# A transformer block with conditioned norm: attention rebuilt batch by batch, scores as fp32 matmuls in four row tiles, and their burst placed ahead of an output projection

## What is computed

```python
emb = silu(sin_emb(timestep)) @ W_ada + b_ada
scale, shift = split(emb[:, None, :], 2, axis=-1)
x = ln(src) * (1.0 + scale) + shift
q, k, v = heads(x @ Wq + bq), heads(x @ Wk + bk), heads(x @ Wv + bv)
scores = einsum('bhqd,bhkd->bhqk', q / sqrt(32), k) + attention_bias   # bias: 64 x 16 x 128 x 128
scores = where(src_mask, -inf, scores)
ctx = merge(einsum('bhqk,bhkd->bhqd', softmax(scores), v))
x = x + (ctx @ Wo + bo)
h = ln(x) * g2 + beta2
out = x + (gelu2(h @ W1 + b1) @ W2 + b2)
```

## Time and profile before

| | |
|---|---|
| median of 3 runs | 2750.17 us (2747.64 to 2753.22) |
| span of the profiled execution | 2749.9 us |
| PE / DVE / ACT / POOL busy | 2608.5 / 1646.0 / 1152.7 / 889.7 us |
| mean granted TensorE clock | 0.991 |
| attention stage, 134 to 1182 us | 28 pairs; DMA engines 58% busy |
| last residual add of attention | 1273.24 us |
| first feed-forward matmul | 1277.87 us |

### The profile page before, as it was taken

How to read it: one execution, slowest core, us unless ns; L and a number is a source line. 1 busy time by engine, 2 the same in 40 slices (tenths; PEclk the granted TensorE clock), 3 DMA queues, 4 the chain that set the end, 5 groups by cost and what they waited for, 6 DMA issues and landing times.

```text
span 2749.9 us, 47237 instructions
## 1 busy us (share of the span) xinstructions
PE 2608.5 (95%) x15386; PEld 2152.0 (78%) x15386; DVE 1646.0 (60%) x3087; ACT 1152.7 (42%) x3625; POOL 889.7 (32%) x767
## 2 busy tenths in 40 slices
PE   5899999999999999987999999999999999999999
PEld 3778777877777878776888888788887887878887
DVE  6899999999999999995423332332233323322322
ACT  3667777767776767774321122112211221112111
POOL 3666666666666666662000000000000000000000
PEclk8999999999999999998999999999999999999999
DMA  6556555556555556553200000000000000000000
GB/s 183 144 155 167 155 144 149 160 155 167 153 146 149 158 156 166 153 151 96 73 20 31 32 14 18 32 31 14 18 31 32 13 19 32 31 10 22 31 16 16
DMA packets 307526, 236.72 MB, mean 86 GB/s; under 512 B 27808, under 2 KB 265504, under 8 KB 303328
## 3 DMA queue, kind: packets, MB, share of 16 engines
q1 hardware_dynamic: 307424, 235.22, 30.5%
HBM read 151.01 MB, written 33.82 MB: 67 GB/s over the span
## 4 chain that ended last, share of the span: by engine, by line
PE 52%; DVE 1%; issue 0%; ACT 0%; DVEq 0%
PE psH L1088 9%; PE psH L1090 9%; PE psH L1089 9%; PE psY L1088 8%; PE psY L1090 8%; PE psY L1089 8%; PE turn L201 1%; DVE hT_hi L219 0%; DVE hT_lo L222 0%; ACT gf L1021 0%; DVE wo_hi L1046 0%; DVE r L1063 0%; DVE w_lo L1053 0%; ACT w_hi L1026 0%; DVEq L953 0%
## 5 line engine op out<-in xcount | busy, mean ns | idle before, releaser
L1021 ACT ACTIVATE gf<-psH,b_c 128x512 f32<-128x512 f32 x256 | 176.2, 688 | 1184.2 <-PE psH L1090 1184.2
L1046 DVE CAST wo_hi<-gf 128x512 fp32r<-128x512 f32 x256 | 109.6, 428 | 925.4 <-ACT gf L1021 925.4
L650 ACT ACTIVATE s<-s,nmx 128x128 f32<-128x128 f32 x1024 | 398.6, 393 | 162.3 <-DVE nmx L715 161.3
L1088 PE MATMUL psH<-hT_hi,w_hi 128*128 128x512 f32 x1024 | 405.9, 396 | 7.3 <-DVE w_lo L1053 5.1
L1088 PE MATMUL psY<-w_hi,wo_hi 128*128 128x512 f32 x1024 | 410.4, 401 | 0.0
L1090 PE MATMUL psH<-hT_hi,w_lo 128*128 128x512 f32 x1024 | 406.0, 396 | 0.0
L1089 PE MATMUL psH<-hT_lo,w_hi 128*128 128x512 f32 x1024 | 405.4, 396 | 0.0
L1090 PE MATMUL psY<-w_hi,wo_hi 128*128 128x512 f32 x1024 | 405.0, 396 | 0.0
L1089 PE MATMUL psY<-w_lo,wo_hi 128*128 128x512 f32 x1024 | 404.4, 395 | 0.0
L586 POOL TENSOR_TENSOR s<-s,rinv 128x512 f32<-128x512 f32 x256 | 266.4, 1040 | 422.8 <-DVE rinv L721 422.8
L580 POOL TENSOR_TENSOR bias<-bias,mneg 128x512 f32<-128x512 f32 x256 | 329.8, 1288 | 2.1 <-DVE mneg L726 2.1
(11 more groups left out here) (152 smaller groups left out, 5356.5 us busy)
## 6 DMA issues: line engine op xcount, KB each, us to landing
bias<-in_bias SPq DMA_DIRECT2D x128, 512.0 KB, 4.9
adab<-ada_rows SPq DMA_DIRECT2D x32, 1024.0 KB, 6.1
kbd<-kT SPq DMA_DIRECT2D x256, 128.0 KB, 2.6
xin<-in_x SPq DMA_DIRECT2D x32, 512.0 KB, 3.8
kbd<-kT SPq DMA_DIRECT2D x256, 64.0 KB, 2.3
resid<-rout SPq DMA_DIRECT2D x64, 256.0 KB, 3.0
r<-resid SPq DMA_DIRECT2D x16, 1024.0 KB, 5.6
out<-r SPq DMA_DIRECT2D x64, 256.0 KB, 2.2
```

The source lines that it names most:

```text
L650: last = act.activation(s[:, g % 2, j, :], s[:, g % 2, j, :], ACT.Exp, bias=nmx[:, g % 2, j:j + 1], accum_out=sums[:, g % 2, j:j + 1])
L1021: act.activation(gf[:, j % 2, :], psH[j % 2][:, :], ACT.Gelu_apprx_sigmoid, bias=b1_c[:, j:j + 1]).then_inc(gelu_done, 1)
L1046: dve.tensor_copy(gT[0][:, j % 2, :], gf[:, j % 2, :]).then_inc(g_hi, 1)
L1088: pe.matmul(out_ap, sh, mh, start=start, stop=False)
```

## The change

Attention goes batch by batch (`t`, 64 of them), a step has all four head groups of one batch, and the loop turns over four pairs. What is different:

- Scores: `kf` and `qf` stay fp32. The columns of Wq and Wk (and of bq, bk) are permuted in the setup, so that partitions 32i to 32i+31 of chunk a hold head 4i + a. `qk` is one burst of 16 fp32 matmuls for a whole batch, contraction 32, with a row tile position i * 32, four row tiles in turn, each to its own PSUM bank psS[i]. `kbd`, `kT`, `qT`, their splits, memsets and the SP transfers are gone. The burst of batch t+1 stands in PE's order behind the V projection and ahead of the output projection of batch t-1.
- The transposes of p go to the same four banks psS, after the scores of the next batch have been read from them; `psP` is gone. p·v is one burst for all 16 heads.
- First norm: gain and shift are applied by POOL (`residual`) and the transposes take that `xres`; from PSUM ACT makes the high part in one copy and DVE the low part in one subtraction. Gains come batch by batch (`load_gains`), x and its normalized form further ahead. The turned gains `adaT` and their transposes in the setup are gone.
- bo is no longer in the shift: POOL adds it to the rows of the feed-forward block (`add_bo`, four per group), and the statistics of the second norm wait for it.
- The weight splits for Q and K in the setup are four instructions each with permuted columns instead of one, and bq and bk arrive in four small transfers each.

```diff
+    def residual(self, pool, q, slot, b):
+        out = self.xres[:, slot, b, :]
+        at_least(pool, self.xn_ready, q * 2 + (b + 1))
+        at_least(pool, self.adab_in[b], (q + 1) * DMA)
+        pool.tensor_tensor(out, self.xn[:, b, :], self.adab[:, b, 0:self.DM], ALU.mult).then_inc(self.res_half, 1)
+        at_least(pool, self.res_half, q * 2 + (b + 1))
+        pool.tensor_tensor(out, out, self.adab[:, b, self.DM:], ALU.add).then_inc(self.res_ready, 1)
...
+    def transpose(self, pe, q, slot, b):
+        at_least(pe, self.res_ready, q * 2 + (b + 1))
+        at_least(pe, self.x_split, q * 2 + b)
...
+    def high(self, act, q, u, b):
         at_least(act, self.xt_done, q * 2 + (b + 1))
+        act.activation(self.xT[u][0][:, :, b * P:(b + 1) * P], self.psX[:, :, :], ACT.Copy).then_inc(self.x_hi, 1)
+    def low(self, dve, q, u, b):
         at = slice(b * P, (b + 1) * P)
+        at_least(dve, self.x_hi, q * 2 + (b + 1))
+        dve.tensor_tensor(self.xT[u][1][:, :, at], self.psX[:, :, :], self.xT[u][0][:, :, at].bitcast(F32),
+                          ALU.subtract).then_inc(self.x_split, 1)
...
+    def add_bo(self, pool, n, u, b):
+        at_least(pool, self.r_in[u], ((n - u) // 2 + 1) * DMA)
+        pool.tensor_tensor(self.r[u][:, b, :], self.r[u][:, b, :], self.bo_bc[:, :], ALU.add).then_inc(self.bo_added, 1)
     def statistics(self, dve, n, u, b):
-        at_least(dve, self.r_in[u], ((n - u) // 2 + 1) * DMA)
+        at_least(dve, self.bo_added, n * self.NB + (b + 1))
         dve.bn_stats(self.st[:, b, :], self.r[u][:, b, :]).then_inc(self.bn_done, 1)
...
-            def spread_k(q, b):
...
+                t = p * 2 + b
+                if on.done:
+                    store(t - 2, b)
+                if on.bias:
+                    load_bias(t + 2, p + 1, b)
+                if on.load:
+                    norm.load(sp, p + 4, u % 2)
+                if on.gains:
+                    norm.load_gains(sp, ada_rows, p + 3, b)
...
+            def step(p, u, b, on):
+                t = p * 2 + b
+                if on.turn:
+                    norm.residual(pool, p + 2, (u + 2) % UNROLL, b)
+                if on.prev:
+                    normalize_p(t - 1, 1 - b, G - 1)
+                if on.mask:
+                    for g in range(G - 1):
+                        add_mask(p + b, 1 - b, g)
+                if on.attn:
+                    normalize_p(t, b, 0)
+                if on.mask:
+                    add_mask(p + b, 1 - b, G - 1)
+                if on.attn:
+                    normalize_p(t, b, 1)
+                if on.stats:
+                    norm.root(pool, p + 3)
+                if on.attn:
+                    normalize_p(t, b, 2)
+                if on.tail and b == 0:
+                    pool.wait_ge(second.bo_in, DMA)
+                    for m in range(second.NB):
+                        second.add_bo(pool, 0, 0, m)
+                    second.root(pool, 0)
...
+            def step(p, u, b, on):
+                t, copy = p * 2 + b, copy_q if b else copy_k
+                kq = (p + 1, (u + 1) % 2)
+                if on.prev:
+                    exps(t - 1, 1 - b, G - 1)
+                if on.proj:
+                    copy(*kq, 0)
+                if on.prev:
+                    copy_pT(t - 1, 0)
+                    copy_pT(t - 1, 1)
+                if on.attn:
+                    exps(t, b, 0)
+                if on.proj:
+                    copy(*kq, 1)
+                if on.prev:
+                    copy_pT(t - 1, 2)
+                    copy_pT(t - 1, 3)
+                if on.proj:
+                    copy(*kq, 2)
+                if on.attn:
+                    exps(t, b, 1)
+                if on.proj:
+                    copy(*kq, 3)
+                if on.turn:
+                    norm.high(act, p + 2, u % 2, b)
+                if on.attn:
+                    exps(t, b, 2)
+                if on.split_o:
+                    act.wait_ge(wo_in, DMA)
+                    act.activation(wo[0][:, :, :], raw_o[:, :, :], ACT.Copy).then_inc(wo_hi, 1)
+                if on.tail and b == 1:
+                    act.wait_ge(q_done, PAIRS * G)
+                    act.wait_ge(second.cols_in, 3 * DMA)
+                    second.copy(act, 0, 0)
+                    second.copy(act, 0, 1)
+                if on.last:
+                    second.copy(act, 0, 2)
+                    second.copy(act, 0, 3)
...
+            def scores(t, p, b, g):
+                heads = slice(HG * g, HG * g + HG)
                 at_least(dve, qk_done, t + 1)
                 at_least(dve, bias_ready[b], p * G + (g + 1))
+                at_least(dve, pt_done, (t - 2) * G + (g + 1))
+                dve.tensor_tensor(s[:, b, heads, :], psS[g][:, :, :], bias[:, b, heads, :], ALU.add).then_inc(score_ready, 1)
+            def highest(t, b, g):
+                heads = slice(HG * g, HG * g + HG)
+                at_least(dve, score_ready, t * G + (g + 1))
+                dve.tensor_reduce(nmx[:, b, heads], s[:, b, heads, :], mybir.AxisListType.X, ALU.max,
                                   negate=True).then_inc(nmax_ready, 1)
...
+            def add_residual(t, q, slot, b):
+                at_least(dve, o_done, t + 1)
                 at_least(dve, r_out[b], q * DMA)
+                dve.tensor_tensor(rout[:, b, :], psD[0][:, :], norm.xres[:, slot, b, :], ALU.add).then_inc(r_ready, 1)
...
+            def step(p, u, b, on):
+                t = p * 2 + b
+                if on.attn:
+                    scores(t, p, b, 0)
+                    scores(t, p, b, 1)
+                if on.done:
+                    add_residual(t - 2, p - 1, (u - 1) % UNROLL, b)
+                if on.last:
+                    second.normalize(dve, 0, 0, 3)
+                if on.mask:
+                    negate_mask(p + b, 1 - b)
+                if on.attn:
+                    scores(t, p, b, 2)
+                    highest(t, b, 0)
+                if on.prev:
+                    invert(t - 1, 1 - b, G - 1)
+                if on.attn:
+                    scores(t, p, b, 3)
+                    for g in range(1, G):
+                        highest(t, b, g)
+                if on.norm:
+                    if b:
+                        norm.normalize(dve, p + 3, (u + 3) % 2, 0)
+                    else:
+                        norm.normalize(dve, p + 2, u % 2, 1)
+                if on.stats:
+                    norm.statistics(dve, p + 3, (u + 3) % 2)
+                if on.attn:
+                    invert(t, b, 0)
+                if on.stats:
+                    norm.spread(dve, p + 3)
+                if on.tail and b == 1:
+                    dve.wait_ge(q_done, PAIRS * G)
+                    second.normalize(dve, 0, 0, 0)
+                    second.normalize(dve, 0, 0, 1)
+                if on.prev:
+                    context(t - 1)
+                if on.attn:
+                    invert(t, b, 1)
+                if on.turn:
+                    norm.low(dve, p + 2, u % 2, b)
+                if on.proj:
+                    add_bv(t + 2, (u + 1) % 2, b)
+                if on.attn:
+                    invert(t, b, 2)
...
-            def qk(p, t, b, g):
-                at_least(pe, score_ready, t - 1)
-                if g == 0:
-                    at_least(pe, kbd_in[b], (p + 1) * (2 * HG * DMA))
+            def qk(t, u, b):
                 if b == 0:
-                    at_least(pe, q_split, p * G + (g + 1))
+                    at_least(pe, k_copied, t * 2 + G)
+                    at_least(pe, q_copied, t * 2 + G)
+                at_least(pe, score_ready, t * G)
+                at_least(pe, pt_copied, (t - 1) * G)
                 at = slice(b * P, (b + 1) * P)
-                for i in range(2):
-                    heads = slice(2 * i, 2 * i + 2)
-                    for part in range(2):
-                        last = pe.matmul(psS[g % 2][:, heads, :], qT[:, g, i, at], kbd[b][:, part, g, heads, :],
-                                         start=(part == 0), stop=(part == 1))
+                for a in range(G):
+                    for i in range(HG):
+                        lanes = slice(i * HD, (i + 1) * HD)
+                        last = pe.matmul(psS[i][:, a, :], qf[lanes, u % 2, a, at], kf[lanes, u % 2, a, at],
+                                         start=True, stop=True, tile_position=(i * HD, 0))
                 last.then_inc(qk_done, 1)
...
+            def transpose_p(t, b, g, more):
+                at_least(pe, prob_ready, t * G + (g + 1))
+                if more:
+                    at_least(pe, score_ready, (t + 1) * G + (g + 1))
+                else:
+                    at_least(pe, pt_copied, (t - 1) * G + (g + 1))
+                for a in range(HG):
+                    last = pe.transpose(psS[g][:, a, :], s[:, b, HG * g + a, :], ident[:, :])
...
+            def pv(t, u, b):
```

(72 more changed lines are left out.)

574 lines of the change are left out of this document (159 added, 415 removed).

## The result

| | before | after |
|---|---|---|
| median, us | 2749.6 | 2566.2 |
| span of the profiled execution, us | 2749.9 | 2564.3 |
| PE / DVE / ACT / POOL busy, us | 2608.5 / 1646.0 / 1152.7 / 889.7 | 2496.1 / 1309.4 / 968.7 / 972.2 |
| mean granted TensorE clock | 0.991 | 0.991 |
| last residual add of attention, first feed-forward matmul | 1273.24, 1277.87 | 1090.17, 1094.80 |

The ratio is 0.933 (0.9315 to 0.9345): 6.7% faster. The forecast was 2590 with its own range 2555 to 2630; the time lies 24 us under it. One of the four runs of the changed kernel took 10558.2 us at a granted clock of 1.00, against 2565.5 to 2566.4 in the other three, and the ratio leaves it out.

The account below looks back on a forecast made before the run. PE and DVE were both held near their ends in attention, PE alone in feed-forward. From 2750 us, 152 for 58 steps, 3 at the start and 6 in the tail, less 1, gave 2590; own range 2555 to 2630.

Parts of the forecast that it names:

- The burst: Score matmuls of one batch on PE: 1.2 us after against 2.1 before, bounds 0.9 to 9.0.
- The loads: Weight loads of the score tiles on PE, 0.189 us each: hidden under matmuls, costed at nothing.
- The step: Attention's period per batch: 16.1 us against 18.72, from 15.8 of PE work plus 0.3; bounds 15.5 and 17.2.
- the one tight wait: PE's last transposes of p waiting for POOL's normalization, 7.1 against 7.0 us into the round; 0.3 us added.
- the chain rival: DVE and POOL operations before the last transposes set the step: period 17.2 us, 2654 us in all; chance 0.12.
- The sum: PE's batch before the change: 16.7 us of work out of 18.72, the 2.0 left being waits.
- The start: Setup ahead of the attention rhythm: operations leave and others come, 3 us saved, bounds 10 either way.
- The tail: Residual add of batch 58 to that of batch 63: 75.2 us before, 69 after, 6 saved, bounds 10 either way.
- the feed-forward: POOL's bo adds delay each group's first statistics by 1.3 us; costs nothing except 1 us in the first group.
- the row tiles that don't run side by side: Score burst on PE takes 3.8 us without overlap: 2751 us, no change; chance 0.06, half of it slower.
- the loads that aren't hidden: Score weight loads not hidden under matmuls: burst 0.9 us longer, 56 us more in all, 2646 us; chance 0.07.
- the slower case: Row tiles one after another, each record paying more than 0.11 us: burst 9.3 at 0.28, about 3090 us; chance 0.05.

Follow-up runs that it names:

- the runs on the old order: Three kernels cut from the kernel before: half the score matmuls left out, 2758.1 us; DVE's subtraction for q's low part left out, 2688.6; both, 2683.0.
- the two runs above: The kernel before with half of its score matmuls left out, 2758.1 us, and with DVE's subtraction for q's low part left out as well, 2683.0 us.
- the halved scores: The kernel before with the low part of K left out of the scores, 8 score matmuls a batch instead of 16: 2758.1 us, ratio 1.0036.
- the lighter DVE: The kernel before with DVE's subtraction for the low part of q left out, 2.8 us less DVE work a batch: 2688.6 us, ratio 0.9779.

## Why the prediction was right, point by point

**The burst** (1.2, bounds 0.9 to 9.0) measured 1.10, and the row it was taken from, the p·v records of the earlier trace rows, was the right one: 1.10 beside 1.01. The estimate of 1.4 by the Trainium skill (TensorE: Matmul & The Clock Gate, Part 3) was too high: less 0.2 for the mode, 32 x 0.11 us of records took 0.9, a factor of 3.9 where the page's, at 512 columns, is 3.07. The order of issue decides how far up the bounds one lands: with the loops exchanged it is 1.6 us more.

**The loads** cost nothing, as costed. Had each round been a load and a matmul, the burst would have taken 0.9 us more. The rule of the Trainium skill (TensorE: Matmul & The Clock Gate, Part 3) that a load overlaps a running matmul only where the row group differs is not what the rows show: a row group gets a record every 0.11 us, and its load lasts 0.186.

**The step** (16.1, bounds 15.5 to 17.2) was 15.85. The work, 15.8, was right to within 0.1. The term that was mis-sized is the 0.3 for "the one tight wait": it was nothing, since there were 0.7 us of slack, and in the batches with a long mask operation 0.5 to none, where I had counted -0.1. My round let the mask take 0.7 each time; it takes 0.22 where no POOL operation runs beside it, as in the row at 718.27 and in 30 of 54 batches, and where it does take 0.7 POOL is done at 6.8, not at my 7.1. The place was the right one: with 1.2 us added there and the mask in its way, every second step (17.4 us) becomes what the chain rival said. The step makes 58 x 0.25 = 14.5 us of the miss.

**Where the 2.87 come from.** The sum took 16.7 of work and 2.0 of waits. In the kernel before, PE's weight loads wait 103.7 us for other engines in 56 batches, 1.85 each; to the two rows comes above all this one:

```profile
PEld turn L126 <- DVE xn L119: 28.3, 28, 1.1
```

So the work before was nearer to 16.9, an estimate (18.72 less 1.85), and it is 15.7 now: 1.2 is work and 1.8 is waits, less 0.1 for the turns of the loop. The larger part was thus never PE's own. I had said that the gain on DVE is what lets the waits go, and the runs on the old order bear it out only in part: with 2.8 of DVE's 5.4 us a batch taken off, 60 us go. How much of the rest is due to the remaining 2.6, to ACT or to the order no run parts.

**The start** (3, bound 10 either way) was 13.4, outside its bound: the largest miss in proportion, and the step behind it had the wrong place. I counted setup operations only. PE's timeline of the kernel before, from its first scores, and then that of the changed kernel:

```profile
64.51 1.22 PE L817 MATMUL psS<-kbd,qT 128*128 128x256 f32 x4 [0.81 <-DMA kbd<-kT]
...
86.48 0.70 PE L825 MATMUL psP<-ident,s 128*128 128x128 f32 x4 [2.86 <-POOL s L586]
...
93.71 0.66 PE L825 MATMUL psP<-ident,s 128*128 128x128 f32 x4 [1.77 <-POOL s L586]
```

```profile
67.15 1.17 PE L779 MATMUL psS<-kf,qf 32*128 32x128 f32 x32
...
81.16 1.17 PE L779 MATMUL psS<-kf,qf 32*128 32x128 f32 x32
```

The first scores come 2.6 us later than before, not 3 earlier: the setup lost. The gain lies behind them, from the first scores to the first residual add: 112.18 - 64.51 = 47.7 before and 98.81 - 67.15 = 31.7 after, 16.0 us. Before, that stretch runs through all slots of a pair and PE stands in it for POOL's p; after, the scores of batch 0 are there in one piece, and its attention is done two steps later. The granted clock has a part in it too. From 60 to 70 us, before and then after, it is 0.50 (the 1.2 GHz level) and 1.00:

```profile
60.00:70.00 10.00, 6.73 (x28) 6.07 (x29) 9.14 (x22) 5.38 (x19) 3.60 (x3) 0.50 0.91 218
```

```profile
60.00:70.00 10.00, 10.00 (x98) 9.09 (x97) 3.43 (x3) 4.26 (x7) 6.24 (x5) 1.00 0.00 0
```

In the old kernel PE was busy for 6.7 of these 10 us, and the V projection that follows starts a matmul every 0.43 us (70.01, 70.44) where full speed has 0.23. From 80 to 90 us the clocks are 0.85 and 1.00. How the 16 us divide among the order, the waits and the clock is not shown. I took the first residual add as the mark for the start and then costed only what lies ahead of the scores.

**The tail** (6, bound 10) was 3.2 and **the feed-forward** (-1) was +2.5. For the latter the cause isn't settled: the kernel before has five waits of PE for the low half of the normalized rows in this block, 2.0 us in all, that the changed one has not, and the two runs above whose feed-forward block is 7 us longer with the same code show how far it moves by itself. The tail has low clocks in both kernels (0.63 from 1240 to 1250 us before, 0.60 from 1060 to 1070 after, within PE's wait of 8.1 us), which the forecast did not price. The bo adds hide as said: from 1200 us on PE is busy for 1359.0 of 1360, while POOL takes them as its rows arrive.

**The chances.** Of the rivals, the row tiles that don't run side by side are refuted by the burst of 1.10 us in rounds of four, the loads that aren't hidden by its rounds of 0.11, the slower case by both. The chain rival came near true in the experiment that adds 1.2 us, not in the change: its distance is 0.7 us in a batch with a short mask operation and less in the others.

| | predicted | measured |
|---|---|---|
| 58 steps | 152 | 166.5 |
| start | 3 | 13.4 |
| tail | 6 | 3.2 |
| behind the last residual add | -1 | 2.5 |
| sum | 160 | 185.6 |

## What to carry to other kernels

Where two engines are near their ends, relieving one of them buys only the part that it alone holds up: in attention the halved scores gave 0.5 us alone and 14 beside the lighter DVE, which gave 61 by itself, and the other 108 of 183 came only with the whole change, after which PE hardly stands. Read such a gain from the stage that was edited: by the whole time the halved scores seemed to cost 10 us, and in the profiles all that was added (6.9 us) lay in a stage that the edit did not touch. So count the work of the engine that is to be the bound, lay the others' operations along one of its rounds, and look at the place where one must be done within tenths of a us; once the right place is found, its slack decides. A batch with extra duties must be laid out too, not the mean one. Put a burst whose outcome others need ahead of a piece of work that nobody waits for: the same instructions, up to 70 us.

## What the runs showed of the hardware

- fp32 row tiles of 32 rows and 128 columns run four side by side if neighbouring instructions go to different row groups and banks: 1.10 us for 32 records, 2.74 if four matmuls in a row go to the same ones. The 128-column weight loads, 186 ns, stay hidden.
- Some DVE operations stretch while POOL works. The mask operation takes 0.22 us alone and up to 1.20 beside a POOL operation (rows above). In the changed kernel the normalization of x and one of the smallest operations of the statistics, both beside POOL's mask adds now, grew from 0.54 and 0.16 us:

```profile
L119 DVE TENSOR_SCALAR xn<-xin,mean,rstd 128x512 f32<-128x512 f32 x55 | 89.2, 1622 | 0.0
...
L57 DVE TENSOR_TENSOR part<-part 128x2 f32<-128x2 f32 x27 | 32.1, 1190 | 0.9
```

  Others don't: the maxima take 0.675 us on average and the score adds 0.677 in the changed kernel (0.686 and 0.680 before), though POOL's mask adds run beside the maxima. Here DVE had the room; a busy time of DVE read off one order is not that of another.
- A turn of the loop costs PE 0.85 (the row at 701.62) to 1.3 us (7.8 in six turns) once PE waits for nothing else, and more with the burst last. No run takes the loop out of the kernel before.
